# A graph network on one core: when SyncE sends node rows, index rows and attributes in the edge phase

## The reference

```python
h = jax.nn.silu(edge_rbf @ W1 + b1)                 # 8 attributes of an edge -> 128
weights = (h @ W2 + b2).reshape(-1, NODE_DIM, LMAX + 1)
node_j = node_feats[col]                            # a node row for each edge
messages = (node_j[:, :, None] * weights).sum(axis=-1)
aggregated = jax.ops.segment_sum(messages, row, num_segments=n_nodes)
self_out = node_feats @ Wself + bself
combined = jnp.concatenate([self_out, aggregated], axis=-1)
return combined @ Wcat + bcat
```

## Time and profile before

| | |
|---|---|
| median of three runs | 8828.42 us (8804.64 to 8845.58) |
| profiled execution: its time, its span | 8759.47 us, 8757.8 us |
| edge phase in it | 119 to 3083 us |
| TensorE, VectorE, ScalarE, GpSimd busy | 4632.7, 3945.9, 1957.3, 5182.5 us |
| mean granted TensorE clock | 0.691 |

### The profile page before, as it was taken

The page is one execution under the profiler, slowest core; times in us unless marked ns, Lnnn a source line. Parts: engine busy times, 40 slices in busy tenths (PEclk is TensorE's granted clock), DMA queues, the critical chain, the costliest instruction groups (busy, mean ns, idle before and its releaser), DMA issues.

```text
span 8757.8 us, 104658 instructions
## 1 busy us (share of the span) xinstructions
PE 4632.7 (53%) x25832; PEld 3934.2 (45%) x25832; DVE 3945.9 (45%) x9762; ACT 1957.3 (22%) x6764; POOL 5182.5 (59%) x5537
## 2 busy tenths in 40 slices
PE   5887877877777888232222323222433343434338
PEld 4766766766666778132222322222322232323234
DVE  6555555566666677333232423223422222222238
ACT  2222222322222200211111111111221121212127
POOL 3665655655555654646666666666366666666651
PEclk7766767777777789566566565666666666666669
DMA  3222322333333377312222122222122222222224
GB/s 106 94 96 86 98 87 91 115 111 111 111 112 110 102 226 209 85 36 48 48 47 48 41 48 46 48 47 48 39 60 62 61 60 62 61 60 62 60 66 156
DMA packets 947907, 715.26 MB, mean 82 GB/s; under 512 B 602516, under 2 KB 811623, under 8 KB 946767
## 3 DMA queue, kind: packets, MB, share of 16 engines
q0 software_dynamic: 163632, 347.28, 13.7%
q1 hardware_dynamic: 266514, 271.53, 10.6%
q10 hardware_dynamic: 517265, 90.70, 5.8%
HBM read 545.12 MB, written 170.28 MB: 82 GB/s over the span
## 4 chain that ended last, share of the span: by engine, by line
another core or an unknown queue 29%; DVE 13%; issue 11%; DVEq 5%; PE 5%; ACT 1%; ACTq 0%; DMA 0%; POOL 0%; SPq 0%; POOLq 0%
DVE acc_b L1683 6%; DVE acc_a L1683 6%; PE bank L2019 3%; DVEq L425 3%; DVEq L1683 2%; PE bank L2065 1%; DVE acc_a L403 0%; ACT acc_a L996 0%; DVE arena L1677 0%; ACT acc_b L996 0%; PE bank L2112 0%; DVE acc_a L1548 0%; DVE arena L1753 0%; DVE arena L1761 0%
## 5 line engine op out<-in xcount | busy, mean ns | idle before, releaser
L807 POOL DMA_INDIRECT arena<-x1d,edge x3322 | 3147.2, 947 | 1804.0 <-issue 963.4
L747 POOL DMA_INDIRECT msgs<-arena x1664 | 1761.2, 1058 | 1304.7 <-issue 957.3
L2065 PE MATMUL bank<-arena 128*128 x7040 | 1347.4, 366 | 2179.0 <-DVE acc_b L1683 1422.2
L2065 PEld LDWEIGHTS bank<-arena 128*128 128x128 f32 x7040 | 1247.7, 272 | 2314.5 <-issue 2302.3
L1677 DVE TENSOR_TENSOR arena<-bank,arena 128x1024 f32<-128x1024 f32 x440 | 538.1, 1223 | 2964.0 <-remote 2651.1
L1040 ACT ACTIVATE arena<-edge,arena 128x1 f32 x3520 | 728.0, 282 | 2644.0 <-issue 1411.9
L1944 PE MATMUL bank<-w2s,acc_b 128*128 128x128 f32 x3328 | 685.7, 368 | 17.1 <-issue 16.2
L1944 PEld LDWEIGHTS bank<-w2s,acc_b 128*128 128x128 f32 x3328 | 580.1, 262 | 147.8 <-issue 147.5
L1926 PE MATMUL bank<-arena 128*128 (+1 forms) x3328 | 635.6, 351 | 3.4 <-issue 2.4
L1683 DVE TENSOR_TENSOR acc_b<-acc_b,bank 128x129 f32 x1760 | 508.7, 289 | 214.9 <-remote 7.8
L1683 DVE TENSOR_TENSOR acc_a<-acc_a,bank 128x129 f32 x1760 | 508.7, 289 | 207.1 <-issue 4.3
(11 more groups left out here) (335 smaller groups left out, 5446.6 us busy)
## 6 DMA issues: line engine op xcount, KB each, us to landing
arena<-rows SPq DMA_DIRECT2D x208, 512.0 KB
arena<-x1d,edge POOLq DMA_INDIRECT x3322
arena<-msgs SPq DMA_DIRECT2D x320, 136.0 KB, 3.2
arena<-msgs ACTq DMA_DIRECT2D x320, 136.0 KB, 3.3
acc_b<-msgs SPq DMA_DIRECT2D x288, 136.0 KB
msgs<-arena POOLq DMA_INDIRECT x1664
pred<-arena ACTq DMA_DIRECT2D x98, 256.0 KB
arena<-pred SPq DMA_DIRECT2D x12, 1792.0 KB, 8.6
```

Source lines behind the costliest of these rows:

```text
L747: pool.indirect_dma_start(msgs, bass.IndirectOffsetOnAxis(ap=pos[:, b, j:j + 1], axis=0), mrow[:, b, j, :], None).then_inc(scattered[b], 16)
L807: pool.indirect_dma_start(grow_t[:, sl, 0:D], None, x1d, bass.IndirectOffsetOnAxis(ap=edge2[:, odd * RING + sl, 1:2].bitcast(i32), axis=0) ...
L2065: last = mm(sum_at(q, k), oh1[:, q % 2, k, :], grow[:, bass.ds(rows_at[q * TG + k], CW)], start=True, stop=True)
```

## The change

SyncE's order of issue changes; what is sent, the waits' conditions for each transfer, and all other engines' programs stay. `edge_loads` now sends, for group g, its window of node rows, then the index rows of group g + 1, then the attributes of group g + 2. The first index rows and the first two groups' attributes are sent ahead of the loop, and the last two pairs are written out.

```diff
-                for b in range(2):
-                    g = 2 * it + b
-                    need(sp, s["wsel_ready"], g - 1)
-                    sp.dma_start(rowsb[:, b, :, :], rows3[bass.ds(g, 1), 0:2, :].to_broadcast([P, 2, GE])).then_inc(rows_in[b], 16)
-                    need(sp, s["attr_cut"], g - 1)
...
-                        sp.dma_start(attr[:, b, :], edge_attr[bass.ds(g * GE, GE), :].rearrange("(p j) a -> p (j a)", j=TG)).then_inc(attr_in[b], 16)
                     need(sp, s["xj_ready"], 2 * g - 2)
...
                     window(0, win_in[b])
 
+                    if not ending or g + 1 < NG:
+                        need(sp, s["wsel_ready"], g)
+                        index_rows(g + 1, 1 - b)
+                    if not ending or g + 2 < NG:
+                        sp.wait_ge(s["attr_cut"], g + 1)
+                        if ending and g + 2 == NG - 1:
+                            last_attributes(b)
+                        else:
+                            attributes(g + 2, b)
...
+            index_rows(0, 0)
+            for b in range(2):
+                attributes(b, b)
             edge_loads(0)
```

More of the change, by code:

```diff
@@ L490, in node_rows, with index_rows, attributes, last_attributes @@
                 sp.dma_start(xpart_x, xwin[bass.ds(it * P - P, P), :]).then_inc(x_staged[0], 16)
-            def edge_loads(it, last=False):
+            def index_rows(g, b):
+                sp.dma_start(rowsb[:, b, :, :], rows3[bass.ds(g, 1), 0:2, :].to_broadcast([P, 2, GE])).then_inc(rows_in[b], 16)
+            def attributes(g, b):
+                sp.dma_start(attr[:, b, :], edge_attr[bass.ds(g * GE, GE), :].rearrange("(p j) a -> p (j a)", j=TG)).then_inc(attr_in[b], 16)
+            def last_attributes(b):
+                av = attr[:, b, :].rearrange("p (j a) -> p j a", a=A)
+                e0 = (NG - 1) * GE
+                sp.dma_start(attr[0:LP, b, :], edge_attr[e0:e0 + LP * TG, :].rearrange("(p j) a -> p (j a)", j=TG)).then_inc(attr_in[b], 16)
+                if LJ:
+                    sp.dma_start(av[LP:LP + 1, 0:LJ, :], edge_attr[E - LJ:E, :].rearrange("(p j) a -> p j a", p=1)).then_inc(attr_in[b], 16)
+                    sp.dma_start(av[LP:LP + 1, LJ:TG, :], edge_attr[0:TG - LJ, :].rearrange("(p j) a -> p j a", p=1)).then_inc(attr_in[b], 16)
+                r = LP + (LJ > 0)
+                sp.dma_start(attr[r:P, b, :], edge_attr[0:(P - r) * TG, :].rearrange("(p j) a -> p (j a)", j=TG)).then_inc(attr_in[b], 16)
@@ L493, in edge_loads @@
+            def edge_loads(it):
                 sp.load(regs, winrow[bass.ds(it * 2 * TG, 2 * TG)].rearrange("(o t) -> o t", o=1))
+                ending = isinstance(it, int) and it >= NG // 2 - 2
                 for b in range(2):
                     g = 2 * it + b
-                    need(sp, s["wsel_ready"], g - 1)
-                    sp.dma_start(rowsb[:, b, :, :], rows3[bass.ds(g, 1), 0:2, :].to_broadcast([P, 2, GE])).then_inc(rows_in[b], 16)
-                    need(sp, s["attr_cut"], g - 1)
@@ L559, in _ @@
                 early_rows(whole, pair)
-            with sp.Fori(IE + 2 * whole + 2, NG // 2 - 1) as it:
+            with sp.Fori(IE + 2 * whole + 2, NG // 2 - 2) as it:
                 edge_loads(it)
-            edge_loads(NG // 2 - 1, last=True)
+            edge_loads(NG // 2 - 2)
+            edge_loads(NG // 2 - 1)
             sp.wait_ge(scattered[0], 16 * TG * (NG // 2))
```

## The result

The changed kernel takes 8739.98 us (median of 4 runs, 8730.84 to 9456.72; the run of 9456.72 us was disturbed and is left out of the ratio), the kernel before 8837.0 us in the same series (4 runs, 8804.64 to 8860.75). The ratio is 0.9889, with a 95% interval of 0.9847 to 0.9931: about 97 us faster. I had predicted 8839 us and a range that ended at 8770. The forecast was wrong, and the case that came true is the one I called "VectorE is the last to arrive".

The account below looks back on a forecast made before the run. The prediction took the edge phase as a ring of TensorE and VectorE whose pace TensorE sets. Its terms, -9 + 24 - 4 = +11 us on 8828 us, gave 8839 us, with a range of 8770 to 8905 us.

Parts of the forecast that it names:

- VectorE is the last to arrive: Faster rival, second stage: in groups without a wait VectorE arrives last; 8778 us at half its upper end, chance 0.22.
- The attributes, -9 us: Edge phase, second stage: attributes sent one group earlier save 0.4 us in each of 23 groups, 9 us less.
- So TensorE sets it, also where the record shows no wait: Second stage: TensorE sets the time from VectorE's position copy to first L1371, even without recorded wait; attribute gain near nothing.
- 13.84, 13.89 and 13.91 us: Three second-stage groups: times from position copy L1507 to next first L1371, with VectorE waits there of 3.06, 0.50 and none.
- The upper end: Second stage: most the earlier attributes could save, 139 us, from 23 groups without a wait at L1371.
- The message tiles, +24 us: SyncE's queue behind odd group's window: tiles go 1.2 us later, TensorE pays in 20 of 48 pairs, 24 us more.
- The start, -4 us: Start of the edge phase: group 1's attributes go ahead of a register load and group 0's window, 4 us less.
- The first stage, nothing: First stage: earlier attributes gain nothing; the 76.8 us of attribute waits go, the 448.0 us at L1371 grow instead.
- The rule on the clock: Skill's rule beside the faster rival: DMA waits idling TensorE lower its clock, closing them restores it; no size given.
- The slower one: Slower rival, SyncE's queue behind odd window: all 48 pairs pay for late message tiles; 8873 us, 8930 at most, chance 0.25.

Follow-up runs that it names:

- second_before: The kernel before, repeated with one added register instruction per awaited value behind the edge phase, on the 7.58 ms kind of chip; 7577.07 us, ratio 0.9992.
- attr_alone: The kernel before with only the attributes sent one group earlier, index rows where they were; 8763.28 us, ratio 0.9886 to the kernel before.
- hold_six: The changed kernel with six scratch scans on VectorE in each even group of the second stage; 8874.99 us, ratio 1.0065 to the kernel before.
- again_before: The kernel before, repeated with one added register instruction per awaited value behind the edge phase; 8867.7 us, ratio 1.0001 to the kernel before.
- again_after: The changed kernel, repeated with the same added register instructions; 8769.89 us, ratio 0.9895 to the kernel before.
- rows_alone: The kernel before with only the index rows sent earlier, attributes where they were; 8884.08 us, ratio 1.0025 to the kernel before.
- tiles_first: The changed kernel with the odd group's index rows and attributes sent behind node rows and message tiles; 8718.09 us, ratio 0.9872 to the kernel before.
- second_after: The changed kernel, repeated on a chip of the 7.58 ms kind; 7502.15 us, ratio 0.9883 to the kernel before.
- tiles_split: The changed kernel with table load and even slot's three message tiles ahead of the odd group's window; ratio 0.9648 to the kernel before (7583.77 us there).

## Why the prediction was wrong

- **The attributes, -9 us.** The step that failed is "So TensorE sets it, also where the record shows no wait", drawn from 13.84, 13.89 and 13.91 us. The third distance was VectorE's own and the second was so but for its last 0.50 us: there VectorE started to cut the attributes 9.5 and 9.8 us after the copy, and some 4 us of its work stand behind them. The first, with 3.06 us of wait, did not end with VectorE's work and was equal by chance. In second_before, where VectorE is always last, the mean distance is 14.06 us too: 10.16 us to the attributes (standard deviation 1.4) and 3.90 us from there (0.09, so no wait in between in any group). Measured: attr_alone is 103.5 us below the kernel before on its chip, less the start some 100 us for the attributes, where I took 9. hold_six shows the step from the other side: delay VectorE there by work alone, and the time comes back.
- **The upper end.** 23 groups x 6.03 us counted only groups without a wait at L1371. By the profile they are 19 (15 even, 4 odd), and in again_before no more than 6, though its second stage is 93.8 us longer than again_after's: six waits of 6 us can't give that. So the test "no wait left at L1371" doesn't pick out the groups that pay. TensorE stood for the copy at L1911 in 38 and 41 of the even groups, and the gain, 1.5 and 2.0 us a pair on average, is bounded by what comes next in each. How the cost arises in a group in which VectorE still waits for a late signal was not shown.
- **The message tiles, +24 us.** ScalarE's wait grew as forecast, to 7.3 us a pair; the tiles went 2.1 us later behind the window, not 1.2. The price is of the right order, if it is there: rows_alone costs 17 to 22 us, and on this kind of chip attr_alone and tiles_first put it at 7 to 15 us, inside the intervals. On the 7.58 ms kind ScalarE started on the tiles 2.65 us later behind the copy, and they took most of the removed wait.
- **The start, -4 us.** 3.5 us measured; in again_before and again_after 140.6 to 136.9.
- **The first stage, nothing.** Not contradicted on the chips of the forecast's kind, where single profiles differ by 28 us and more. On the other kind early attributes alone gave 16 to 19 us there, where VectorE had no wait left in 24 of 51 even groups, though the whole change did not.
- **The rivals.** The faster one had the mechanism and, at half of its upper end, 8778 us; it got 0.22 and ended at 8740. The rule on the clock that I set aside beside it gave the change nothing: the granted clock of the second stage stayed (0.78 in again_before and again_after) on this kind of chip and fell on the other. The slower one did not decide on either kind of chip, but its place, SyncE's queue behind the odd window, turned out to hold the cause of both waits.
- **The range** ended at 8770 since it went to the middle of the rival. The measured time lies between that middle, 8778 us, and the rival's end, 8709 us.

## What to carry to other kernels

Before calling one engine of a ring the bound, read the waits of the engine that is said to set it: a bound engine doesn't stand still at the place where it takes over from the other. Equal distances prove nothing unless the stretches in between are taken apart, and "issue" in front of an instruction that has several waits in the program may hide the other engine: compare the end of each idle time with the end of the instruction that it may have waited for. When two engines wait at the same time for transfers of one queue, look in that queue for the common stretch (here two register reads from DRAM, some 3 to 3.6 us each) before moving the transfers one by one; and measure the better version on more than one chip.

## What the runs showed of the hardware

The chips are of two kinds for this program, and the same kernel differs by 1.28 ms between them. The page of again_before, then of second_before:

```profile
span 8862.1 us, 104878 instructions
PE 4632.5 (52%) x25832; PEld 3931.2 (44%) x25832; DVE 3943.6 (44%) x9762; ACT 1957.5 (22%) x6764; POOL 5195.8 (59%) x5537
```

```profile
span 7579.8 us, 104878 instructions
PE 4646.6 (61%) x25832; PEld 4004.6 (53%) x25832; DVE 3939.5 (52%) x9762; ACT 1911.9 (25%) x6764; POOL 5198.8 (69%) x5537
```

The busy times are equal within 2.5%; all the difference is idle time. On the slower kind it carries a name, the releaser "remote": all waits of the profile under it add up to 5287 us in the kernel before, 5806 in the one after, 5408 in hold_six, and to none in second_before, second_after and tiles_split. The chain that ended last says the same, again_before and then second_before:

```profile
another core or an unknown queue 29%; DVE 13%; issue 11%; PE 5%; DVEq 5%; ACT 1%; ACTq 0%; DMA 0%; POOL 0%; SPq 0%; POOLq 0%
```

```profile
POOL 33%; issue 15%; PE 9%; DVE 2%; ACT 1%; DMA 1%; DVEq 1%; POOLq 0%; SPq 0%; ACTq 0%
```

In the edge phase of the changed kernel such a wait lasts up to 11.4 us at L1389. Where VectorE waited at the first L1371 of a group of the second stage, it started 1.92 us behind the recorded end of TensorE's places in the kernel before (median of 77, at most 7.9 us), and 0.11 us behind it in second_before (46, at most 0.5 us). What lies between the end and the start on the slower kind is open. The phases are longer there (a first stage of 1385 to 1444 us against 1122 to 1142), and the gain of the split tiles is 0.7% against 3.5%; that the late starts cause either was not tested.
